# Circulant product behind quartered loads: matrices and activations through one queue, depth index outermost

## What is computed

```python
def _L0_attn_ref(x, bind_key, unbind_key, gate, decay):
    bound = _circ_conv(x, bind_key)           # irfft(rfft(x) * rfft(key))
    d = jax.nn.sigmoid(decay)
    ...
    decay_matrix = jnp.where(causal, d ** jnp.maximum(diff, 0.0), 0.0)
    hologram = jnp.einsum('ts,bsd->btd', decay_matrix, bound)
    retrieved = _circ_corr(hologram, unbind_key)
    return x + gate * retrieved

def _L0_ffn_ref(x, w_gate, w_up, w_down):     # w_*: int32, times 1/127
    ...
    h = jax.nn.silu(gate) * up
    return jnp.einsum('bsh,dh->bsd', h, wd)

x = L0_attn_x                                 # (8, 2048, 1024) float32
x = x + _layernorm(_L0_attn_ref(_layernorm(x), ...))
x = x + _layernorm(_L0_ffn_ref(_layernorm(x), ...))
```

## Time and profile before

| | us |
|---|---|
| median of 3 runs (lowest, highest) | 818.55 (817.53, 820.23) |
| the profiled execution | 819.04 |
| its span, slowest core (core 0) | 817.5 |
| spans of the eight cores | 812.2 to 817.5 |
| TensorE busy in the span | 672.3 (82%) |
| VectorE busy | 248.8 (30%) |
| ScalarE busy | 209.6 (26%) |

### The profile page before, as it was taken

One profiled execution on the slowest core, in us unless ns is written; L12 is line 12 of the kernel. 1 busy time (PEld: TensorE's weight loads), 2 busy tenths in 40 slices (PEclk: granted clock), 3 DMA queues, 4 the chain that ended last, 5 costly groups with the idle time before them and its releaser, 6 DMA issues.

```text
span 817.5 us, 8441 instructions; the slowest of 8 cores (812.2 to 817.5 us)
## 1 busy us (share of the span) xinstructions
PE 672.3 (82%) x3030; PEld 298.1 (36%) x3030; DVE 248.8 (30%) x595; ACT 209.6 (26%) x309; POOL 29.3 (4%) x58
## 2 busy tenths in 40 slices
PE   0392998997303899799999999598999999999993
PEld 0140322443102344344444444343444444444441
DVE  0078220455564226222222032223222222211223
ACT  2031422334424220311122122514222111213222
POOL 1000000000000000000000000000000000000000
PEclk9996655999755899899999999699999999999998
DMA  8798900000011144244444111014344444400111
GB/s 132 155 327 154 158 20 1 0 1 1 1 27 25 26 78 73 43 68 75 78 78 78 26 51 53 1 51 102 60 74 78 76 77 77 78 0 26 52 53 77
DMA packets 12281, 53.40 MB, mean 65 GB/s; under 512 B 1376, under 2 KB 1376, under 8 KB 11728
## 3 DMA queue, kind: packets, MB, share of 16 engines
q0 software_dynamic: 7632, 36.08, 26.4%
q1 hardware_dynamic: 4608, 16.78, 5.8%
HBM read 80.12 MB, written 8.39 MB: 108 GB/s over the span
## 4 chain that ended last, share of the span: by engine, by line
PE 68%; DVE 10%; DMA 7%; issue 7%; ACT 5%; SPq 1%; DVEq 0%; POOL 0%; ACTq 0%; POOLq 0%
PE pg L637 19%; PE pu L645 19%; PE pu L714 10%; PE pf L714 10%; PE pb L359 4%; DMA cubb<-cuT 4%; ACT t1a L434 2%; DVE sqd L413 2%; DMA x<-xin 2%; PE pt L574 2%; DMA wgu<-wgu 2%; ACT t1a L406 2%; PE pb L354 1%; DVE sta L539 1%; DVE x2t L578 1%
## 5 line engine op out<-in xcount | busy, mean ns | idle before, releaser
L637 PE MATMUL pg<-x2t,wgu 128*128 128x512 bf16 x768 | 177.4, 385 | 10.6 <-DVE xw L664 5.3
L645 PE MATMUL pu<-x2t,wgu 128*128 128x512 bf16 x768 | 173.6, 379 | 0.0
L658 ACT ACTIVATE sil<-pg,z 128x512 bf16<-128x512 f32 x96 | 65.4, 687 | 242.3 <-PE pg L637 242.3
L637 PEld LDWEIGHTS pg<-x2t,wgu 128*128 128x128 bf16 x768 | 75.0, 99 | 106.9 <-issue 22.9
L645 PEld LDWEIGHTS pu<-x2t,wgu 128*128 128x128 bf16 x768 | 75.2, 98 | 90.6
L664 DVE SCALAR_TENSOR_TENSOR xw<-sil,pu 128x512 bf16<-128x512 bf16 x64 | 43.7, 688 | 168.7 <-PE pu L645 166.6
L476 PE MATMUL pr<-hc,zt 128*128 128x512 bf16 x256 | 62.1, 386 | 7.6 <-ACT t1a L406 6.6
L714 PE MATMUL pu<-wdtb,xw 128*128 128x512 bf16 x256 | 60.2, 390 | 0.0
L714 PE MATMUL pf<-wdtb,xw 128*128 128x512 bf16 x256 | 57.9, 379 | 2.1 <-DVE hc L664 2.1
L237 PE MATMUL cp<-cubb,cbtb 128*128 128x512 bf16 x128 | 31.3, 412 | 33.6 <-DMA cubb<-cuT 33.6
L664 DVE SCALAR_TENSOR_TENSOR hc<-sil,pu 128x512 bf16<-128x512 bf16 x32 | 22.0, 688 | 88.9 <-PE pu L645 88.9
(11 more groups left out here) (93 smaller groups left out, 438.7 us busy)
## 6 DMA issues: line engine op xcount, KB each, us to landing
wgu<-wgu POOLq DMA_DIRECT2D x48, 512.0 KB, 5.4
x<-xin SPq DMA_DIRECT2D x16, 512.0 KB, 13.8
out<-x SPq DMA_DIRECT2D x16, 512.0 KB, 2.7
wdtb<-wdt POOLq DMA_DIRECT2D x1, 6144.0 KB, 41.1
cbtb<-cbt POOLq DMA_DIRECT2D x1, 2048.0 KB, 18.0
cubb<-cuT POOLq DMA_DIRECT2D x1, 2048.0 KB, 29.6
cstf_s<-cstf POOLq DMA_DIRECT2D x1, 257.0 KB, 3.4
cstb_s<-cstb POOLq DMA_DIRECT2D x1, 128.0 KB, 2.9
```

The lines of the kernel that those rows point to most:

```text
L637: pe_g[eta][c] = op("tensor", lambda e, sl=sl, c=c, d=d: e.matmul(PG[sl][:, 512 * c:512 * c + 512], WGU[sl][:, 128 * d:128 * d + 128], X2T ...
L645: pe_u[eta][c] = op("tensor", lambda e, sl=sl, c=c, d=d: e.matmul(PU[sl][:, 512 * c:512 * c + 512], WGU[sl][:, 1024 + 128 * d:1024 + 128 * ...
L658: sc_sil[eta][c] = op("scalar", lambda e, sl=sl, c=c: e.activation(SIL[sl][:, 512 * c:512 * c + 512], PG[sl][:, 512 * c:512 * c + 512], AF ...
```

## The change

- The `cbt` and `cuT` loads are cut into four quarters of 2048 columns (two blocks k each). The `x` loads move from SP's queue to POOL's, where the order is now, four times over: a quarter of `cbt`, a quarter of `cuT`, four tiles of `x`. All six loads of a group count on that group's semaphore `LDX` to `LDX4`, which is complete at 96. Nothing waits between the groups, and `wdt` follows without a wait.
- `CP` has eight PSUM banks in place of four. The 16 outputs are made in two halves of eight. In each half k is the outer loop and g the inner one; in the first half each k waits for the group of loads that holds it. The evictions of a half follow all its matmuls in the program. The second half waits for the eighth eviction of the first.
- The statistics of `x` stand in a loop of their own, with the same instructions, and wait for 96.

```diff
-    w("sync", "WCC", 32)
-    for t in range(TN):
-        dma("sync", X[t][:], xin[:, 1024 * t:1024 * t + 1024], f"LDX{t // 4 + 1}".replace("LDX1", "LDX"))
     ldx_tot = [4 * 16] * 4
 
-    dma("gpsimd", CBTB[:], cbt[:, :], "WCC")
-    wt_ccin = dma("gpsimd", CUBB[:], cuT[:, :], "WCC")
-    for gname in ("LDX", "LDX2", "LDX3", "LDX4"):
-        w("gpsimd", gname, 64)
+    for q in range(4):
+        gsem = f"LDX{q + 1}".replace("LDX1", "LDX")
+        dma("gpsimd", CBTB[:, 2048 * q:2048 * q + 2048], cbt[:, 2048 * q:2048 * q + 2048], gsem)
+        dma("gpsimd", CUBB[:, 2048 * q:2048 * q + 2048], cuT[:, 2048 * q:2048 * q + 2048], gsem)
+        for t in range(4 * q, 4 * q + 4):
+            dma("gpsimd", X[t][:], xin[:, 1024 * t:1024 * t + 1024], gsem)
     wt_wd = dma("gpsimd", WDTB[:], wdt[:, :], "WWD")
...
-    CP = [pa.enter_context(nc.psum_tensor(f"cp{i}", [128, 512], F32)) for i in range(4)]
-
-    w("tensor", "WCC", wt_ccin)
+    CP = [pa.enter_context(nc.psum_tensor(f"cp{i}", [128, 512], F32)) for i in range(8)]
...
-    for g in range(16):
-        dj, fc = g // 2, g % 2
-        if g >= 4:
-            w("tensor", "SC", dv_ccevac[g - 4])
+    for half in range(2):
+        g0 = 8 * half
+        if half == 1:
+            w("tensor", "SC", dv_ccevac[7])
         for k in range(ND):
-            pe_cc[g] = op("tensor", lambda e, dj=dj, fc=fc, k=k, g=g:
-                          e.matmul(CP[g % 4][:], CBTB[:, 1024 * k + 128 * dj:1024 * k + 128 * dj + 128],
...
+            if half == 0:
+                w("tensor", f"LDX{k // 2 + 1}".replace("LDX1", "LDX"), 96)
+            for g in range(g0, g0 + 8):
+                dj, fc = g // 2, g % 2
+                pe_cc[g] = op("tensor", lambda e, dj=dj, fc=fc, k=k, g=g:
+                              e.matmul(CP[g % 8][:],
...
-        t = g
         if t % 4 == 0:
-            w("vector", f"LDX{t // 4 + 1}".replace("LDX1", "LDX"), 64)
+            w("vector", f"LDX{t // 4 + 1}".replace("LDX1", "LDX"), 96)
```

More of the change, by code:

```diff
@@ L230, in build_nc @@
     last_chain_end = {0: 0, 1: 0}
-    for g in range(16):
-        dj, fc = g // 2, g % 2
-        if g >= 4:
-            w("tensor", "SC", dv_ccevac[g - 4])
+    for half in range(2):
+        g0 = 8 * half
+        if half == 1:
+            w("tensor", "SC", dv_ccevac[7])
         for k in range(ND):
-            pe_cc[g] = op("tensor", lambda e, dj=dj, fc=fc, k=k, g=g:
-                          e.matmul(CP[g % 4][:], CBTB[:, 1024 * k + 128 * dj:1024 * k + 128 * dj + 128],
[L238 to L244, removed]
+            if half == 0:
[4 more added lines that the diff above has]
+                              e.matmul(CP[g % 8][:],
+                                       CBTB[:, 1024 * k + 128 * dj:1024 * k + 128 * dj + 128],
+                                       CUBB[:, 1024 * k + 512 * fc:1024 * k + 512 * fc + 512],
+                                       start=(k == 0), stop=(k == ND - 1)),
+                              "PE" if k == ND - 1 else None)
+        for g in range(g0, g0 + 8):
+            dj, fc = g // 2, g % 2
+            w("scalar", "PE", pe_cc[g])
+            dv_ccevac[g] = op("scalar", lambda e, dj=dj, fc=fc, g=g:
+                              e.activation(HC[dj][:, 512 * fc:512 * fc + 512], CP[g % 8][:],
+                                           AF.Identity, bias=0.0, scale=1.0), "SC")
+    for t in range(TN):
         if phases <= 0.77:
             continue
-        t = g
         if t % 4 == 0:
-            w("vector", f"LDX{t // 4 + 1}".replace("LDX1", "LDX"), 64)
+            w("vector", f"LDX{t // 4 + 1}".replace("LDX1", "LDX"), 96)
         p = 12 * (t % 2)
```

## The result

| | before | after |
|---|---|---|
| median, us | 818.48 (10 runs) | 831.21 (9 runs) |
| ratio, 95% interval | | 1.0149 (1.013 to 1.0168) |
| profiled execution, us | 819.04 | 833.18 |
| its span, slowest core | 817.5 (core 0) | 831.6 (core 3) |
| spans of the eight cores | 812.2 to 817.5 | 818.2 to 831.6 |

The change makes the kernel 12.7 us slower by the medians and 12.2 by the ratio; 831 was forecast. Some executions of a program on eight cores are slower with a lower clock on one die; the medians contain them, the ratios leave them out. Between two groups the ratios are the better comparison; each has an interval of 0.12 to 0.27% either way, 1 to 2 us.

The account below looks back on a forecast made before the run. The bound was the wait for the last x tiles, then VectorE work, then the scan; the product had 8.8 us slack. Loads win 3.9 us, product loses 15.5: 819.04 + 11.6, plus 0.5 for the clock, written 831, range 827 to 838.

Parts of the forecast that it names:

- the sum: Scan start moves from 64.39 + 16.34 to 60.5 + 31.8 = 92.3: loads win 3.9, product loses 15.5, net +11.6 us.
- T4: Time at which the last load group, LDX4, is complete: forecast 60.5 us, bounds 58 to 64.4, before 64.39.
- rival A: The software queue carries x slower: 835 if the hole is filled again, 837 at 260 GB/s; chance 15%.
- Steps 1 and 2: Product's first half: first eviction at T4 + 4.1, eight ScalarE evictions 4.4 us, done T4 + 8.6; TensorE idles 2.5.
- Step 3: Product's second half: 64 matmuls at 0.216 us each, then eight bare evictions of 4.4 us, ending at T4 + 25.5.
- one of my signs of being wrong: The product's second half takes much more than 14 us.
- Rival B: Product's second half at the low clock: 833 if it falls and rises once (2.3 us), 844 if throughout; chance 12%.
- The 0.5 us that I added for a clock of 0.81: Allowance for the product running some us at that granted clock, some 0.05 us more per matmul.
- Step 4: VectorE's hc and xw take 6.3 us as before, scan at T4 + 31.8; statistics, needing T4 + 10.0, no longer late.
- A shift of the start is a shift of the end: Everything after the scan's start keeps its length; scan start to first L476 matmul 60.0 and 59.9 us on two cores.
- my own sign (more than 1 us): Prediction is wrong if the stretch from the scan's start to the end changes by more than that.
- rival C: Faster: the scan's 24 later groups run at the higher clock, 18.2 us come back, 813 in place of 831; chance 4%.

Follow-up runs that it names:

- the first experiment: Kernel before the change, with x in 16 loads over POOL's queue right behind the two whole matrices, old loop: 815.49 against 819.49 us, ratio 0.994.

## Why the prediction was right, point by point

**The time.** 831 forecast, 831.21 measured, within 827 to 838. The direction and the mechanism came out: 80 matmuls and two rows of evictions moved behind the last `x`. That the total agrees to 0.2 us is luck. In the profiled execution, which the sum was made for, 830.6 was forecast and 833.18 measured: a term of 2.3 us was missing and another was 1.0 too small, against 0.5 too much for T4; the median of the changed kernel then came out 2.0 below its profiled execution.

- *T4.* Forecast 60.5, within 58 to 64.4. Measured 60.0 on core 3, 60.8 on core 0. The early groups at 21.4, 33.9 and 47.6, forecast about 20, 33.5 and 47. Right, and rival A is out: in the first experiment `x` on the software queue runs at 335 GB/s where the hardware queue had 335.
- *Steps 1 and 2.* First eviction forecast T4 + 4.1, measured 64.12 - 60.02 = 4.1. Eight evictions forecast 4.4, measured 4.03. TensorE's idle time forecast 2.5, measured 2.27.
- *Step 3.* Forecast T4 + 25.5 for the last eviction. Measured 86.55 - 60.02 = 26.5 on core 3. The clock was not held there: 0.57 from 68 to 72, and a second half of 15.65 us, which was one of my signs of being wrong. On five of eight cores it was 13.97, as forecast (core 0). Rival B in its small form, 1.7 us where I had priced 2.3, came true on three cores. The 0.5 us that I added for a clock of 0.81 is not seen: at 13.97 us 64 matmuls take 0.218 each.
- *Step 4.* Here a step is missing. I took VectorE's statistics as done at T4 + 10, a number read between 64.39 and 74.43 that already held the table load and the square root (72.16 to 73.76 in the kernel before). VectorE's own part was done at T4 + 7.7; the square root is on ScalarE, and in ScalarE's list it stands behind all sixteen evictions. In the kernel before this cost nothing, since the last eviction ended 6.6 us ahead of it. After the change it waits for the last eviction, with a table load of 1.28 us: `hc` starts at 88.84, 2.3 us after the last eviction. The experiment that moved it gave 1.9 us of time and 2.5 us from T4 to the scan. The change's diff shows the order; I had followed VectorE's and TensorE's lists past the moved evictions, and not ScalarE's.
- *The sum.* T4 to scan: 31.8 forecast, 33.2 to 35.1 measured. Start of the scan over the eight cores: 79.6 us on average before, 93.7 after, a shift of 14.1, where 11.6 was forecast. My base, 80.73, was that of core 0, 1.1 later than the average, so the loads win 2.8 us and not 3.9, though T4 itself was right. The profiled executions differ by 14.1 as well (819.04 and 833.18).
- *A shift of the start is a shift of the end.* True of what follows the scan (from the first L476 matmul to the end 675.2 us on average before, 674.6 after), and false of the scan, which I had argued from two cores. I took two cores of one execution with 60.0 and 59.9 us for the scan and called the length one. It has at least four: 60, 54, 52 and 46 us, by how much of its chunks runs at the higher clock. In the changed kernel's profile two cores of eight had 53.9, 6 us less than before, which by my own sign (more than 1 us) was wrong. So rival C, the scan at the higher clock, is no rival of the whole kernel but a draw for each core, and the slowest of the eight cores has some 60 us in every profile except the two with the scan's waits filled. The medians differ by 12.7 and the profiled executions by 14.1: the profiled one of the changed kernel lies 2.0 us over its median. I put this to these draws: in its execution of 830.55 us a single core has a span of 829.0 at a clock of 0.897, and the other seven, at 0.905 or more, have 811.9 to 820.6. The scan's length was not traced there, so this is argued, not shown.

**What the experiments add.** The two halves of the change, taken apart: one queue is worth -4.0 us with the old loop behind whole matrices (-4.9 by the ratio), the new loop is worth 0 by itself. It is only `x` between the quarters that costs, 15 to 17 us between two kernels that differ in the order of their loads. By the average start of the scan the split is -2.8 for the loads (76.8 with `x` behind the matrices, 79.6 before) and +16.9 for the rest (93.7), where the forecast had -3.9 and +15.5.

**The clock and the queue.** On core 3 the early bursts that followed waits of 6.0 and 8.3 us took 5.42 us each, where 16 matmuls at the higher clock take 3.61. The Trainium skill, in "TensorE: Matmul & The Clock Gate", section "HAM oscillation — how this bites in real kernels", describes bursts between waits for DMA that each start at the low clock. This case's traces agree (a mean clock of 0.74 from 33 to 47 us). A burst that is hidden costs nothing. The one at T4 is not: its first eviction came after 4.1 us, and after 2.2 in the kernel with the quarters first, whose last burst ran at the higher clock (33.95 to 36.15, core 5); the sum had this from rows. The fall of the clock between the halves, where TensorE waits for ScalarE and not for a DMA, cost 1.7 us on three cores. The Trainium skill, in "DMA: Bandwidth & Descriptors", section "SWDGE vs HWDGE vs iDMA", sends plain loads to the hardware queue and calls it faster to set up. No run here shows a gain from it: tiles of half a megabyte ran at 335 GB/s over either queue from 51 to 58 us.

## What to carry to other kernels

Mixing two inputs in one queue can make each consumer as late as the last piece of both; put what has the longer work behind it first, whole, and the input whose work keeps pace with its arrival behind it. When evictions or other instructions are moved, follow every engine's list past them, also for the small instruction of another stage that now stands behind. And where the slowest of several cores sets the time, compare all cores' lengths of a stage, in more than one execution, before calling it constant.

## What the runs showed of the hardware that I had not expected

- A stretch of eight one-column matmuls and a TensorE wait of 1.82 us, with one-row matmuls behind it, was followed on most cores by a chunk at the lower clock, 12.6 to 13.3 us on core 0 in place of 7.7. With seven matmuls of 512 columns in the wait the clock was 1.00 from 90 to 122 us on all eight cores, and the time fell by 18 us. Between dense matmuls a wait of 1.59 us did no such thing; waits of 1.7 to 2.8 us between the halves of the product cost some cores the clock and others not.
- The same program gives single cores spans of 790.3 and 810.1 us in one execution: 14.7 of these 19.8 us are the scan, at 45.9 and 60.6 us.
- Two DMA queues at once share unevenly: 8.39 MB of casts were released 35 us after the start beside `x` on the other queue, 28.5 alone, and the sum of both was ready somewhat earlier than from one queue (58.3 to 59.6 us, where one queue had 59.6 to 61.5).
- Eight evictions of 128x512 back to back took 4.03 us. With 0.60 for one alone that is one every 0.49 us, where the row of four that I had used gives 0.54.
